# One attention and routing kernel: GpSimd splits the projections of Q and K, the weighted sum runs three steps behind instead of two, and VectorE takes five of the copies that ScalarE made

## The reference, cut to what matters

```python
qh = (q @ Wq.T).reshape(B, 512, 16, 16).transpose(0, 2, 1, 3)      # q: layernorm(x)
kh = (k @ Wk.T).reshape(B, 1601, 16, 16).transpose(0, 2, 1, 3)     # k = v = ctx_1024
vh = (v @ Wv.T).reshape(B, 1601, 16, 16).transpose(0, 2, 1, 3)
attn = softmax(einsum('bhnc,bhlc->bhnl', qh * D**-0.5, kh), axis=2)
attn = attn / sum(attn, axis=-1, keepdims=True)
out = einsum('bhnl,bhlc->bhnc', attn, vh) ... @ Wo.T
x = x + tanh(g_xattn) * out
x = x + tanh(g_ffn) * experts(layernorm(x))                        # router, top 2 of 8, gelu
```

## Time and profile before

| | |
|---|---|
| median of 3 runs | 1864.9 us (1862.82 to 1866.27) |
| the profiled execution | 1863.19 us, its span 1861.3 us |
| granted TensorE clock, mean | 0.977 |
| TensorE matmul, VectorE, ScalarE, GpSimd busy | 1665.0, 1408.8, 1281.1, 557.7 us |
| first exponential of batch 0 and last of batch 7 | 56.3 and 1270.3 us after the start |

### The profile page before, as it was taken

One profiled execution on the slowest core, in us unless ns is written; L12 is line 12 of the kernel. 1 busy time (PEld: TensorE's weight loads), 2 busy tenths in 40 slices (PEclk: granted clock), 3 DMA queues, 4 the chain that ended last, 5 costly groups with the idle time before them and its releaser, 6 DMA issues. The chain is left out here.

```text
span 1861.3 us, 31293 instructions
## 1 busy us (share of the span) xinstructions
PE 1665.0 (89%) x9775; PEld 892.7 (48%) x9888; DVE 1408.8 (76%) x2269; ACT 1281.1 (69%) x3634; POOL 557.7 (30%) x837
## 2 busy tenths in 40 slices
PE   5789899999988999999999998876399999999997
PEld 3223333333323333333333332213399999999997
DVE  1599999999999999999999999994444444444442
ACT  1699999999999999999999999993011111111111
POOL 5142152243225235234323422213122222222222
PEclk8899999999999999999999999997699999999999
DMA  4914512611721651371272162206322222222222
GB/s 153 228 40 128 156 39 85 197 56 52 205 70 57 153 141 39 114 192 39 68 196 62 57 166 73 80 29 252 108 37 37 34 37 37 37 37 36 37 34 29
DMA packets 124933, 168.64 MB, mean 91 GB/s; under 512 B 14320, under 2 KB 102256, under 8 KB 124816
## 3 DMA queue, kind: packets, MB, share of 16 engines
q1 hardware_dynamic: 102064, 136.77, 26.8%
q0 software_dynamic: 13344, 17.90, 5.7%
q10 hardware_dynamic: 9408, 12.58, 1.8%
HBM read 117.96 MB, written 49.24 MB: 90 GB/s over the span
## 5 line engine op out<-in xcount | busy, mean ns | idle before, releaser
L675 ACT ACTIVATE w_all<-scores,negmax 128x512 f32<-128x512 f32 (+1 forms) x1664 | 1126.8, 753 | 33.3 <-DVE negmax L826 27.5
L826 DVE TENSOR_REDUCE negmax<-scores 128x2 f32<-128x1024 f32 (+1 forms) x832 | 1001.6, 1215 | 81.5 <-PE scores L565 74.3
L565 PE MATMUL scores<-q_stack,w_all 128*128 128x512 bf16 (+1 forms) x1551 | 478.1, 384 | 68.8 <-ACT w_all L675 54.1
L675 ACT ACTIVATION_READ_ACCUMULATOR w_all<-scores,negmax 128x1 f32 (+1 forms) x1664 | 453.6, 273 | 0.0
L578 PE MATMUL acc<-w_all,vz 128*32 128x512 f32 (+1 forms) x3328 | 443.5, 605 | 4.1 <-POOL vz L950 3.9
L1144 ACT ACTIVATE hidden<-ps_hidden 128x512 f32<-128x512 f32 x142 | 84.8, 597 | 428.9 <-PE ps_hidden L1107 428.9
L565 PEld LDWEIGHTS scores<-q_stack,w_all 128*128 128x128 bf16 (+1 forms) x1664 | 115.9, 99 | 529.7 <-ACT w_all L675 401.3
L950 POOL TENSOR_TENSOR vz<-w_all,rz 128x68 f32<-128x68 f32 (+1 forms) x416 | 124.6, 300 | 806.5 <-DVE rz L812 787.4
L1107 PEld LDWEIGHTS ps_hidden<-rows_t,w_sb 128*128 128x128 f32 x2272 | 266.2, 193 | 5.7 <-DVE rows_t L1171 1.7
L1107 PE MATMUL ps_hidden<-rows_t,w_sb 128*128 128x128 f32 x2272 | 267.0, 276 | 1.2 <-DVE rows_t L1171 1.2
L1120 PE MATMUL ps_y<-w_sb,hidden 128*128 128x256 f32 x1136 | 256.8, 380 | 0.0
(11 more groups left out here) (134 smaller groups left out, 1040.2 us busy)
## 6 DMA issues: line engine op xcount, KB each, us to landing
w_all<-k_parts SPq DMA_DIRECT2D x256, 200.1 KB, 3.5
q_stack<-q_parts SPq DMA_DIRECT2D x256, 64.0 KB, 3.3
w_all<-in_ctx_t SPq DMA_DIRECT2D x8, 1601.0 KB, 7.2
k_parts<-parts SPq DMA_DIRECT2D x42, 300.0 KB, 2.8
w_all<-in_w ACTq DMA_DIRECT2D x12, 1024.0 KB, 12.0
rows<-routed SPq DMA_DIRECT2D x71, 129.0 KB, 2.1
q_parts<-parts SPq DMA_DIRECT2D x14, 384.0 KB, 3.1
k_parts<-parts SPq DMA_DIRECT2D x14, 300.8 KB, 3.2
```

The source lines that it names most:

```text
L565: mm = pe.matmul(scores[0:r, 2 * (u % SLOTS) + j % 2, :], k_stack[:, g, j, lt * P:lt * P + r], q_stack[:, g, j, :], start=True, stop=True)
L675: e = act.activation(probs[0:r, s % RING, j, :], scores[0:r, 2 * (u % SLOTS) + j % 2, :], ACT.Exp, bias=negmax[0:r, u % 4, j % 2:j % 2 + 1 ...
L826: dve.tensor_reduce(negmax[0:r, u % 4, :], scores[0:r, 2 * (u % SLOTS):2 * (u % SLOTS) + 2, :], AX.X, ALU.max, negate=True).then_inc(negma ...
```

## The change

Four things change, all in the attention stage and outside the prologue.

1. For Q and K, ScalarE copies the bank to `resid` in float32 and frees the bank by that. VectorE has no part in it any more. GpSimd makes the high part, subtracts it from `resid` in place, makes the middle part and subtracts it into the low part: four instructions a chunk, two in the fill's step and two in the next, with waits on its own semaphore `split_step`. The wait for the store of the parity buffer moves from ScalarE to GpSimd. ScalarE waits for the parts of the chunk two before (`parts_ready`), whose `resid` it writes over.
2. VectorE takes V fills 1, 3 and 5 and both `x_turn` (`DVE_TAKES`), behind the second reduction and the reciprocals of the step.
3. `weigh` runs `LAG` = 3 steps behind the scores. `take_acc` moves one step later with it.
4. In `FILL_AT`, `o_turn` 0 moves from step 16 to 18 and K chunk 5 from 18 to 17, `o_turn` 1 moves from 29 to 33, and Q 0 and Q 1 from 31 and 33 to 30 and 32.

```diff
+LAG = 3
-    15: ("next", "k", 4), 16: ("cur", "o_turn", 0), 18: ("next", "k", 5), 19: ("tail", "row_turn", 0),
+    15: ("next", "k", 4), 17: ("next", "k", 5), 18: ("cur", "o_turn", 0), 19: ("tail", "row_turn", 0),
...
+DVE_TAKES = {("v", 1), ("v", 3), ("v", 5), ("x_turn", 0), ("x_turn", 1)}
...
-                    if s >= 2 and it.cur:
-                        weigh(it.b, s - 2)
+                    if s >= LAG and it.cur:
+                        weigh(it.b, s - LAG)
...
+                    act.wait_ge(parts_ready, (b + 1) * CHUNKS + at - 1)
+                    act.activation(resid[:, at % 2, 0:n], spare[:, 0:n], ACT.Copy,
+                                   scale=D ** -0.5 if name == "q" else 1.0).then_inc(fill_taken, 1)
...
-                elif name in ("attn_turn", "row_turn"):
+                elif name in ("attn_turn", "row_turn", "x_turn"):
...
+                        on_act = ("v", "x_turn") if it.first else ("v", "x_turn", "q", "k")
+                        if f and (f[0] not in on_act or not it.first and f in DVE_TAKES) and p == (f[0] in ("q", "k", "v", "x_turn")):
                             take(it, *f)
...
+            def split(it, at, n, part, k):
+                done = 3 * (it.b * CHUNKS + at)
+                if k == 1:
+                    pool.wait_ge(split_step, done + 2)
+                pool.tensor_tensor(part[:, k, 0:n], resid[:, at % 2, 0:n], zero[:, 0:1].to_broadcast([P, n]),
+                                   ALU.add).then_inc(split_step, 1)
+                pool.wait_ge(split_step, done + (1, 3)[k])
+                if k == 0:
+                    pool.tensor_tensor(resid[:, at % 2, 0:n], resid[:, at % 2, 0:n], part[:, 0, 0:n],
+                                       ALU.subtract).then_inc(split_step, 1)
...
+                            wait(pool, parts_stored[c % 2], ((b + 1) * (CHUNKS // 2) + at // 2) * 16)
+                            split(it, at, n, parts_of(it, c), 0)
```

More of the change, by code:

```diff
@@ L71 @@
     7: ("tail", "out_proj", 0), 9: ("tail", "out_proj", 1), 11: ("next", "k", 2), 13: ("next", "k", 3),
-    15: ("next", "k", 4), 16: ("cur", "o_turn", 0), 18: ("next", "k", 5), 19: ("tail", "row_turn", 0),
+    15: ("next", "k", 4), 17: ("next", "k", 5), 18: ("cur", "o_turn", 0), 19: ("tail", "row_turn", 0),
     20: ("tail", "row_turn", 1), 22: ("tail", "logits", 0), 24: ("next", "k", 6), 26: ("next", "k", 7),
-    27: ("next", "x_turn", 0), 28: ("next", "x_turn", 1), 29: ("cur", "o_turn", 1), 31: ("next", "q", 0),
-    33: ("next", "q", 1), 35: ("next", "v", 0), 37: ("next", "v", 1), 38: ("tail", "prefix", 0),
+    27: ("next", "x_turn", 0), 28: ("next", "x_turn", 1), 30: ("next", "q", 0), 32: ("next", "q", 1),
+    33: ("cur", "o_turn", 1), 35: ("next", "v", 0), 37: ("next", "v", 1), 38: ("tail", "prefix", 0),
     40: ("next", "v", 2), 42: ("next", "v", 3), 44: ("next", "v", 4), 46: ("next", "v", 5),
@@ L319, in attention_and_routing @@
         middle_ready = sem("middle_ready")
+        split_step = sem("split_step")
         parts_ready = sem("parts_ready")
@@ L594, in run @@
                         unit_scores(it.b, s, 1)
-                    if s >= 2 and it.cur:
-                        weigh(it.b, s - 2)
-                    if s < 2 and it.tail:
-                        weigh(it.b - 1, STEPS + s - 2)
+                    if s >= LAG and it.cur:
+                        weigh(it.b, s - LAG)
+                    if s < LAG and it.tail:
+                        weigh(it.b - 1, STEPS + s - LAG)
             over_batches(pe, run)
@@ L614, in take @@
                 b = it.b
-                if name in ("q", "k"):
+                if name in ("q", "k") and not it.first:
                     c, at, n = it.chunk(name, i)
                     act.wait_ge(fill_ready, it.made(name, i))
-                    if not it.first:
-                        wait(act, parts_stored[c % 2], ((b + 1) * (CHUNKS // 2) + at // 2) * 16)
+                    act.wait_ge(parts_ready, (b + 1) * CHUNKS + at - 1)
+                    act.activation(resid[:, at % 2, 0:n], spare[:, 0:n], ACT.Copy,
+                                   scale=D ** -0.5 if name == "q" else 1.0).then_inc(fill_taken, 1)
+                elif name in ("q", "k"):
+                    c, at, n = it.chunk(name, i)
+                    act.wait_ge(fill_ready, it.made(name, i))
                     act.activation(parts_of(it, c)[:, 0, 0:n], bank(it, name, i)[:, 0:n], ACT.Copy,
@@ L659, in run @@
                 for s in range(STEPS):
-                    if s < STEPS - 1 and it.fill(s) and it.fill(s)[0] != "logits":
+                    if s < STEPS - 1 and it.fill(s) and it.fill(s)[0] != "logits" and (it.first or it.fill(s) not in DVE_TAKES):
                         take(it, *it.fill(s))
@@ L716, in take @@
                 dve.wait_ge(fill_ready, it.made(name, i))
-                if name in ("attn_turn", "row_turn"):
-                    to = {"attn_turn": attn_t, "row_turn": row_t}[name]
+                if name == "v":
+                    if i == 0 and b > 0:
+                        dve.wait_ge(vz_ready, b * STEPS)
+                    m = min(2, LT - 2 * i)
+                    r = rows_of(2 * i) if m == 1 else P
+                    dve.tensor_copy(v_ones[0:r, (b + 1) % 2, 2 * i:2 * i + m, :, 0:DH],
+                                    spare[0:r, 0:m * D].rearrange("p (t h c) -> p t h c", t=m, h=H)).then_inc(fill_taken, 1)
+                elif name in ("attn_turn", "row_turn", "x_turn"):
+                    to = {"attn_turn": attn_t, "row_turn": row_t, "x_turn": x_t}[name]
                     dve.tensor_copy(to[:, i, :], spare[:, :]).then_inc(fill_taken, 1)
@@ L827, in run @@
                                               AX.X, ALU.max, negate=True).then_inc(negmax_ready, 1)
-                        if p == 1 and s == 1 and it.tail:
+                        if p == 1 and s == LAG - 1 and it.tail:
                             take_acc(b - 1, G - 1)
-                        if p == 1 and it.cur and s in (LT + 1, 2 * LT + 1, 3 * LT + 1):
+                        if p == 1 and it.cur and s in (LT + LAG - 1, 2 * LT + LAG - 1, 3 * LT + LAG - 1):
                             take_acc(b, s // LT - 1)
@@ L990, in run @@
                         c, at, n = it.chunk(name, i)
-                        pool.wait_ge(middle_ready, (b + 1) * CHUNKS + at + 1)
+                        if it.first:
+                            pool.wait_ge(middle_ready, at + 1)
+                        else:
+                            split(it, at, n, parts_of(it, c), 1)
                         pool.tensor_tensor(parts_of(it, c)[:, 2, 0:n], resid[:, at % 2, 0:n], parts_of(it, c)[:, 1, 0:n],
@@ L999, in run @@
                         pool.wait_ge(fill_taken, it.made(name, i))
-                        pool.tensor_tensor(parts_of(it, c)[:, 1, 0:n], resid[:, at % 2, 0:n], zero[:, 0:1].to_broadcast([P, n]),
-                                           ALU.add).then_inc(middle_ready, 1)
+                        if it.first:
+                            pool.tensor_tensor(parts_of(it, c)[:, 1, 0:n], resid[:, at % 2, 0:n], zero[:, 0:1].to_broadcast([P, n]),
+                                               ALU.add).then_inc(middle_ready, 1)
+                        else:
+                            wait(pool, parts_stored[c % 2], ((b + 1) * (CHUNKS // 2) + at // 2) * 16)
+                            split(it, at, n, parts_of(it, c), 0)
                     if it.tail and STEPS - 2 * NT <= s:
```

1 line of the change is left out of this document (removed).

## The result

The changed kernel takes 1886.3 us (median of four runs, 1884.9 to 1888.96) against 1865.6 us in the same comparison: a ratio of 1.0117 (1.0102 to 1.0131), 20.7 us slower where 9.3 us faster were forecast. The time lies outside the range. The profiled execution took 1888.96 us, its span 1887.2.

What follows compares the result with a forecast made beforehand. ScalarE's queue was taken as the bound, VectorE close behind. -2.35 - 2.4 + 2.0 + 1.65 = -1.1 us in each of six batches, -2.75 in batch 0, 0 in batch 7: -9.3, giving 1855.6 us, range 1837 to 1874.

Steps and rivals of the forecast that it cites:

- ScalarE's copies: ScalarE's queue: three V and two x copies leave it, 0.47 us each, -2.35 us a batch.
- The bank freed earlier: Q and K fills: TensorE's waits on `resid` go, -2.4 us a batch, between 0 and 3.3 possible.
- VectorE, +2.0, with 3.0 as its upper bound: VectorE's five copies fall in other steps than the dropped resid work: +2.0 us a batch, bounds 0 and 3.0.
- this wait: TensorE waiting on the bank for VectorE's new copies beyond its room; named as something that would make the prediction wrong.
- GpSimd, steps 13 to 21: The split at 1.84 us a step makes `vz` late: +1.65 us a batch, bounds -1.7 and +3.5; lag needed, not enough.
- The waits that the prediction itself forecast for TensorE: Around step 20 TensorE waits for `vz`, which would come up to 5 or 6 us after its reciprocal.
- the slow one: Rival: in steps 13 to 21 GpSimd holds the step rate for longer, 1867 to 1874 us; chance 0.24.
- 2.1 us per pair of the split: Slow rival's price on GpSimd instead of 1.84; with the reciprocal as late as now, steps 13 to 21 cost +3.5 us.
- The one in which VectorE becomes the bound: Rival: the five copies cost their full 3.0, half the waits return, nothing moves, 1861 to 1868 us; chance 0.16.
- The last batch: Batch 7 has no fills for a next batch: change 0, period staying at 141.2 us.
- The rule of the Trainium skill: Two-input elementwise work is about twice as slow on GpSimd: 4.8 us of VectorE traded for about 18, change should lose.
- the rows' reading: GpSimd's slower split matters only where it has no gap, six steps of 52.

Runs made afterwards that it cites:

- e1: The changed kernel, but ScalarE makes the five V and x copies again (DVE_TAKES empty): 1867.5 us, ratio 1.0029 to the kernel before.
- e4: The changed kernel, but VectorE makes its V and x copies behind the first reduction of the step: 1865.3 us, ratio 1.0011.
- e7: The changed kernel with CENTRE_X = 21, x copies back on ScalarE, V 1, 3, 5 on VectorE behind the first reduction: 1847.7 us, ratio 0.9914.
- e5: The changed kernel with all five copies on ScalarE, x normalised in steps 21 to 24, and LAG = 2: 1870.8 us, ratio 1.0034.
- e2: The changed kernel with CENTRE_X = 21, so GpSimd normalises the next x in steps 21 to 24, not 17 to 20: 1871.7 us, ratio 1.0048.
- e9: The changed kernel with two extra matmuls on TensorE in each of steps 17 to 21: 1884.3 us, ratio 1.0118.
- e12: The kernel of e11 with the extra matmuls of e9 in steps 17 to 21: 1870.0 us, ratio 1.0043.
- e11: The changed kernel with both x copies back on ScalarE, V 1, 3, 5 still on VectorE behind the second reduction: 1876.6 us, ratio 1.0083.
- e10: The kernel of e7, with GpSimd making the second copy of the normalised rows in steps 27 and 28, not 15 and 16: 1839.7 us, ratio 0.9872.

## Why the prediction was wrong, point by point

**ScalarE's copies, -2.35 us a batch.** Right: the starts show 0.465 us for each, and the float32 copy of a K chunk holds the queue for the same 0.385 as the bf16 one.

**The bank freed earlier, -2.4.** Right in kind, a little large. Steps 0 to 12 went from 3.7 to 2.2 us in the changed kernel, and steps 24 to 51 from 1.3 to 0.7 when ScalarE has all copies (e1): -2.1.

**VectorE, +2.0, with 3.0 as its upper bound.** This step failed. It measured +4.9 (5.6 against 0.7 in e1): 2.3 us in steps 27 to 29, where the sum had 0.9, and 2.6 in the V steps and around them, where it had 1.1. I had counted the throughput of VectorE only, and so took 3.0 as the end. The copy also holds the only fill bank, and it stands last in its step. I named this wait among the things that would make the prediction wrong, but gave it no price, although shows its price for `resid`, which stood at the same place in the step. The runs split the 4.9: 2.5 us for the place in the step (e4), and 2.4 that stay with the early place. That these 2.4 are VectorE's load is argued and not shown; of them the V copies have 0.7 by e7.

**GpSimd, steps 13 to 21, +1.65.** The sum held: 23.61 against 23.7 us, and steps 13 to 23 grew by 2.0 us in batch 2. That the lag is needed is shown by e5 (3.0 us a batch without it, with x normalised late), and that it is not enough by e2 (1.9 us come back once room is made).

**What was not in the sum at all.** The clock, a second failed step: the sum put it at nothing, with no reason given. The waits that the prediction itself forecast for TensorE let it fall to 1.2 GHz (e9 and e12 show this for step 20; for step 29 it is read from the place alone, and from e11, where nothing fell at step 29 once the x copies were gone). Against batch 2, batches 1 and 3 to 6 lost 4.4, 2.9, 1.6, 2.9 and 1.7 us, together 13.4.

Put together, an undisturbed batch: -2.3 - 2.1 + 4.9 + 2.0 = +2.5, as batch 2 shows (155.03 - 152.57). Six of them are +14.8, the clock +13.4, batch 0 gained 1.3 (158.1 before, 156.8 now). That makes +26.9 by this profile, whose span grew by 25.9: the first exponential came 0.9 later (57.20 against 56.30), the last batch was 0.3 shorter and what follows it 1.7 shorter. This profile is of the slowest of the four runs; by the medians the kernel is 20.7 us slower, so the clock's share of that is probably smaller than 13.4; no trace of a median run shows it. Of the rivals, the slow one was nearest in place but not in mechanism, as its price, 2.1 us per pair of the split, did not come: where no `rz` was waited for, a pair for K took at most 1.85 us. The one in which VectorE becomes the bound had the right engine and the wrong size. The last batch stayed about as it was, as said: 140.2 us from its first exponential to its last against 140.5.

The rule of the Trainium skill, page "GPSIMD Engine Reference", section 4.1, on elementwise work on GpSimd, weighed in the prediction, pointed the right way for the changed kernel, though more of its loss came from VectorE's copies, and the wrong way for e10: there GpSimd does the same split, and the kernel is 1.3% faster than before. The measurement decides for the rows' reading: it matters only where GpSimd has no gap.

## What to carry to other kernels

When a copy moves to another engine, price the buffer that it frees: find its place in the new engine's step and who waits for that buffer. Load alone gave 2.0 of the 4.9 us here. When work is added to an engine that is half idle, lay its queue out step by step; the same 73 us a batch cost 2 to 6 us in a crowded stretch and nothing once two other pieces of row work, which nobody waited for, were moved away. And where the sum shows TensorE waiting, add what a fall of its clock would cost (1.6 to 4.4 us each here).

## What was not expected of the hardware

TensorE's granted clock fell to 0.51 for about 10 us in the middle of a steady loop, behind waits for `vz` of 1.08, 0.61 and 2.04 us, in some batches and not in others with the same waits. A fall cost up to 4.4 us of a batch. Two redundant matmuls, together 0.43 us, in each of five steps removed the falls there, and made the kernel 0.4% faster where no other wait let the clock fall (e12 against e11).
